# A graph-network kernel: three of ten scaled one-hot copies move from ScalarE to GpSimd

## The reference

```python
a = leaky_relu(sum((xj + ee) * attn, axis=-1), 0.01)   # one logit per edge
m = segment_max(a, dst, num_segments=N)                # the greatest logit of each target node
a = exp(a - m[dst])
denom = segment_sum(a, dst, num_segments=N)
```

## Time and profile before

| | |
|---|---|
| median of 3 runs | 4138.27 us (4135.9 to 4142.09) |
| span of the profiled execution | 4129.6 us; its own time is not listed apart from the runs |
| busy PE, DVE, ACT, POOL over the span | 78%, 59%, 44%, 27% |
| the phase of the change | about 2013 to 2442 us of the span |

### The profile page before, as it was taken

The page is one execution under the profiler, slowest core; times in us unless marked ns, Lnnn a source line. Parts: engine busy times, 40 slices in busy tenths (PEclk is TensorE's granted clock), DMA queues, the critical chain, the costliest instruction groups (busy, mean ns, idle before and its releaser), DMA issues. The chain is left out here.

```text
span 4129.6 us, 85621 instructions
## 1 busy us (share of the span) xinstructions
PE 3235.8 (78%) x18069; PEld 2388.7 (58%) x18070; DVE 2446.4 (59%) x6689; ACT 1829.5 (44%) x6323; POOL 1134.4 (27%) x908
## 2 busy tenths in 40 slices
PE   5666658998887859999543337989996899998988
PEld 4444437887876746767422226878885444544455
DVE  7999988888765643254688868777764200000554
ACT  1888882344455521021688748777772000000111
POOL 1788888888888401101000000000000000000002
PEclk9999999999999979999655559999998999999999
DMA  2444444678788846757565535444331443542047
GB/s 98 125 120 121 122 104 110 186 231 247 224 259 275 292 156 175 211 169 211 174 192 183 170 105 174 125 121 121 105 104 41 150 149 103 199 157 69 1 179 264
DMA packets 436836, 652.83 MB, mean 158 GB/s; under 512 B 101676, under 2 KB 293015, under 8 KB 436610
## 3 DMA queue, kind: packets, MB, share of 16 engines
q1 hardware_dynamic: 353154, 521.08, 40.7%
q10 hardware_dynamic: 53040, 121.95, 8.2%
q0 software_dynamic: 30544, 8.56, 3.0%
HBM read 439.71 MB, written 210.77 MB: 158 GB/s over the span
## 5 line engine op out<-in xcount | busy, mean ns | idle before, releaser
L1065 POOL DMA_INDIRECT slots<-all_B,put_index x800 | 1042.9, 1304 | 343.2 <-issue 338.0
L1950 POOL MEMSET c_T<- 128x28 f32 x1 | 0.1, 148 | 1983.5 <-POOLq L142 1983.5
L1315 ACT ACTIVATE lm_raised<-lm_hot,srt_words 128x125 f32<-128x125 bf16 x1200 | 356.3, 385 | 83.9 <-DVE lm_top L1230 66.9
L2498 DVE TENSOR_TENSOR upd_pre<-upd_po,upd_bias 125x512 f32<-125x512 f32 x25 | 17.3, 691 | 621.7 <-PE upd_po L2429 621.7
L1349 PE MATMUL lm_ps<-lm_v,lm_node 125*128 x1220 | 170.5, 184 | 267.3 <-DVEq L1217 95.2
L2073 PE MATMUL att_ps<-att_right,att_left 128*125 128x125 f32 x2380 | 314.1, 285 | 70.7 <-ACT att_right L2094 57.7
L1036 PE MATMUL put_ps<-put_right_in,put_left_in 128*128 128x125 f32 x2210 | 319.8, 295 | 63.1 <-ACT put_left_in L893 62.8
L2073 PEld LDWEIGHTS att_ps<-att_right,att_left 128*125 128x125 f32 x2380 | 284.5, 190 | 96.3 <-issue 85.4
L1036 PEld LDWEIGHTS put_ps<-put_right_in,put_left_in 128*128 128x128 f32 x2210 | 281.8, 202 | 87.2 <-ACT put_left_in L893 73.2
L2147 DVE SCALAR_TENSOR_TENSOR att_power<-soft_negated,srt_words,att_far 128x125 f32 (+1 forms) x1190 | 321.0, 344 | 3.8 <-ACT att_right L2094 3.3
L1651 PE MATMUL c_po<-c_halves,c_T 125*125 125x512 f32 x1250 | 320.1, 405 | 0.0
(11 more groups left out here) (418 smaller groups left out, 5816.7 us busy)
## 6 DMA issues: line engine op xcount, KB each, us to landing
c_T<-counts SPq DMA_DIRECT2D x255, 312.5 KB, 3.3
pair<-put_T ACTq DMA_DIRECT2D x125, 625.0 KB
att_ring<-hot SPq DMA_DIRECT2D x480, 160.0 KB
gio_T<-pair SPq DMA_DIRECT2D x60, 1250.0 KB, 5.9
hot<-put_hot SPq DMA_DIRECT2D x448, 160.0 KB
all_A<-in_edge_attr_dram SPq DMA_DIRECT2D x100, 448.0 KB
lm_planes<-src_rows SPq DMA_DIRECT2D x123, 320.0 KB, 3.6
counts<-put_T ACTq DMA_DIRECT2D x125, 312.5 KB
```

What stands on the lines that cost most here:

```text
L1065: nc.gpsimd.indirect_dma_start(slots, bass.IndirectOffsetOnAxis(index[:, C * g + j:C * g + j + 1], 0), stage[:, C * g + j, :], None).then_ ...
L1315: ins = nc.scalar.activation(raised[:, j % 2, c * P:(c + 1) * P], hot[:, j, c * S:c * S + P], ACT.Copy, scale=logit[:, ds(G * g + c, 1)])
```

## The change

ScalarE makes the first seven scaled copies of a group (`LIFTS = 7`). GpSimd makes the other three in one instruction: the product of three one-hot matrices, seen as 128 x 3 x 125 with a step of 128 between chunks, with the three logits of each partition, broadcast along the 125 nodes. A new semaphore `hoisted` counts GpSimd's groups and starts at 3, as `lifted` does. DVE waits for it ahead of the maximum and in the filling loop, SP before it reloads a one-hot slot. GpSimd waits for the same three semaphores as ScalarE.

```diff
--- before.py
+++ after.py
@@ -1143,8 +1143,9 @@
         arrived, flipped, copied, written = (s.sem(n) for n in ("arrived", "flipped", "copied", "written"))
         bounded, gathered, floored, cleared = (s.sem(n) for n in ("bounded", "gathered", "floored", "cleared"))
         split, chain_sem = s.sem("split"), s.sem("chain")
-        expanded, looked, summed, ready, lifted, grouped = (
-            s.sem(n) for n in ("expanded", "looked", "summed", "ready", "lifted", "grouped"))
+        expanded, looked, summed, ready, lifted, hoisted, grouped = (
+            s.sem(n) for n in ("expanded", "looked", "summed", "ready", "lifted", "hoisted", "grouped"))
+        LIFTS = 7
         joined, passed, turned, ended = (s.sem(n) for n in ("joined", "passed", "turned", "ended"))
         PZ = 4
 
@@ -1185,6 +1186,7 @@
                         sp.wait_ge(landed[(j + 1) % RING], 16 * (i + (j + 1) // RING) + 16)
                         sp.sem_inc(arrived, 1)
                         sp.wait_ge(lifted, g + 1)
+                        sp.wait_ge(hoisted, g + 1)
                         sp.sem_inc(passed, 1)
                         if not last or j < 3:
                             load_hot(g + 1, j + 1)
@@ -1225,6 +1227,7 @@
                 def greater(g, first):
                     lift = raised[:, ds(g % 2, 1), :].rearrange("p a n -> p (a n)")
                     dve.wait_ge(lifted, g + 4)
+                    dve.wait_ge(hoisted, g + 4)
                     dve.wait_ge(grouped, g + 2)
                     if first:
                         ins = v.tensor_copy(top8[:, :], lift)
@@ -1311,7 +1315,7 @@
                         act.wait_ge(ready, g + 1)
                         act.wait_ge(hot_arrived, g + 1)
                         act.wait_ge(grouped, g + 1)
-                        for c in range(G):
+                        for c in range(LIFTS):
                             ins = nc.scalar.activation(raised[:, j % 2, c * P:(c + 1) * P], hot[:, j, c * S:c * S + P], ACT.Copy,
                                                        scale=logit[:, ds(G * g + c, 1)])
                         ins.then_inc(lifted, 1)
@@ -1319,6 +1323,17 @@
             @block.gpsimd
             def _(pool):
                 nc.gpsimd.memset(ones[:, :], 1.0).then_inc(cleared, 1)
+                pool.sem_inc(hoisted, 3)
+                with pool.Fori(0, turns_of(pool, k)) as i:
+                    for j in range(RING):
+                        g = RING * i + j
+                        pool.wait_ge(ready, g + 1)
+                        pool.wait_ge(hot_arrived, g + 1)
+                        pool.wait_ge(grouped, g + 1)
+                        by_chunk = (lambda t, w: t.rearrange("p (c n) -> p c n", n=w)[:, :, 0:P])
+                        nc.gpsimd.tensor_tensor(by_chunk(raised[:, j % 2, LIFTS * P:], P), by_chunk(hot[:, j, LIFTS * S:], S),
+                                                logit[:, ds(G * g + LIFTS, G - LIFTS)].unsqueeze(2).to_broadcast([L, G - LIFTS, P]), ALU.mult
+                                                ).then_inc(hoisted, 1)
 
             @block.tensor
             def _(pe):
```

## The result

The changed kernel takes 4153.51 us (median of 5 runs, 4150.27 to 4155.78), against 4138.27 us before: 1.0035 times as long, with a 95% interval from 1.0025 to 1.0046. So the change costs 15.2 us. The forecast had the sign and the mechanism; the time lies in the stated range, but the cost is a third of the 43 us that the sum gave.

A forecast was written before the change was run, and what follows sets the result against it. The prediction took DVE to bound the stretch. A 40.4 us hold and a 2.5 us wait, 43 us, raised the span from 4129.6 to 4172.6; 8.7 carried over gave 4181 us, range 4140 to 4228.

The forecast's parts named there:

- DVE sets the pace and ScalarE's relief is worth nothing: Stretch of ScalarE's copies: DVE's 2.95 us step is the bound; gain at most 0.6 us, counted as zero.
- The extra wait, 2.5 us: Ahead of DVE's maximum: one wait more, uncovered, 119 x 0.021 = 2.5 us; bounds 0 and 5 us.
- The product's own time, 0.80 us: GpSimd's product of 375 elements a partition: 0.175 us fixed plus two passes, 0.80 us; bounds 0.49 and 1.30.
- Two-operand instructions are held until a reading product ends: On DVE, L1232, L1218 and L1222 beside GpSimd's product: held like the early cast, until the product ends.
- The hold, 0.43 us in each of 94 steps, 40.4 us: At DVE's sum L1218: start held from 2109.08 to the product's end at 2109.51; 40.4 us in all.
- 94 collisions: DVE's steps where product and L1218 meet: 119 less the 25 after block ends, where L1281 covers the product.
- the held cast: Trace's first microseconds: a DVE cast of 1000 elements took 7.01 us beside a GpSimd memset, 0.68 us with GpSimd idle.
- free window: Time in a DVE step when both operands' way is free: 0.37 us, against the 0.80 the product needs.
- the likeliest case: DVE held by GpSimd's product: 9 to 90 us slower, 4181 us likeliest, own range 4152 to 4228; chance 0.62.
- slower than any row: Rival on GpSimd's product: above 1.30 us it holds L1218 longer; at 2.2 us, 4313 us; chance 0.11.
- ScalarE did not set the pace: Rival it answers: ScalarE's copies set the pace, so the time could fall as far as 4068 us; chance 0.05.
- nothing to be measured: Rival on DVE: two-operand instructions are not held, or the product fits into 0.37 us; 4143 us; chance 0.22.

The follow-up runs named there:

- e4_dry: Against the kernel before: ScalarE still makes all ten copies, GpSimd adds a product of the same shape on tiles of its own; 4153.96 us, 1.0038.
- e11_both: The change with L1218's sums in PSUM and DVE's wait for hoisted at the head of its step; 4141.4 us, 1.0007 to the kernel before.
- e1_wait_only: The change with GpSimd's loop and waits but no product, ScalarE making all ten copies; 4140.97 us, 1.0005 to the kernel before.
- e10_early_wait: The change with DVE's wait for hoisted moved to the head of its step; 4149.92 us, 1.0028 to the kernel before.
- e6_copy: The change with GpSimd copying 1200 elements in the product's place, ScalarE making all ten copies; 4187.21 us, 1.0115 to the kernel before.
- e7_psum_z: The change with L1218's sums in an idle PSUM bank, so L1220 reads one operand from PSUM; 4141.89 us, 1.0006 to the kernel before.
- e5_write: The change with a GpSimd memset of 1320 elements in the product's place, ScalarE making all ten copies; 4143.22 us, 1.0008 to the kernel before.

## Why the prediction was right in sign and wrong in size

- *DVE sets the pace and ScalarE's relief is worth nothing:* right. e4_dry and the change take the same time with ten and with seven copies on ScalarE, and e11_both returns to about the time of before.
- *The extra wait, 2.5 us:* right within its bounds; 3.4 us of idle time, 0.029 us a step, because the instruction went from 21 to 50 ns and DVE's sequencer has no lead there, as its row suggested. Some 1 us of it comes back elsewhere (e1_wait_only). e10_early_wait shows that the place made the price.
- *The product's own time, 0.80 us:* right; 0.81 undisturbed, 0.835 on the average. The reasoning held too: one pass costs e6_copy's copy about 0.84 ns an element (1.19 us undisturbed, less the fixed 0.18), the product's two passes twice that. The estimate of 0.99 us from the Trainium skill's page "GPSIMD Engine Reference", section 3.1, was too long for this product: with two, three and four copies it takes 625, 835 and 1043 ns, 1.67 ns an element.
- *Two-operand instructions are held until a reading product ends:* right, and shown by e4_dry, e6_copy and e7_psum_z. The Trainium skill's page "SBUF — State Buffer", section "Who interferes with whom", says that a DVE instruction with two SBUF inputs contends with a GpSimd instruction that reads SBUF, not with one that only writes. This case agrees: with GpSimd only writing, e5_write, the two-operand L1222 stayed at 170 ns, and with one operand from PSUM, e7_psum_z, L1220 at 169. Why the two-operand sums of the earlier trace rows were not drawn out beside GpSimd's indirect DMAs, no run here shows.
- *The hold, 0.43 us in each of 94 steps, 40.4 us:* this step failed; it measured 0.15 us in 69 steps, 10.4 us. The mechanism was right and the term mis-sized, in three parts. First, "the product runs from 2108.71", the recorded end of L1210: it was let in 0.15 us before that, which with its true length of 0.81 ends it 1.22 us after L1210's start and not 1.35. That is 0.13 us a step. Second, L1218 "is held to 2109.51" and only then begins: it ends 0.02 us behind the product and not its own 0.17, 0.15 us more. Together 0.28 x 69 = 19.3 us. Third, "94 collisions" counted the 25 steps behind a block's first copy, where the sum comes 0.23 us later against the product and escapes: 25 x 0.43 = 10.8 us. The trace of before has this: there L1218 starts 1.19 us after L1210 does, and 0.92 behind a maximum. 40.4 - 19.3 - 10.8 = 10.3.

The first two parts could have been read in the earlier trace rows: the held cast ended 0.54 us behind the memset and takes 0.68 by itself, so it too had begun to count 0.14 us before the holder's recorded end. The free window that the prediction put at 0.37 us was in effect 0.37 + 0.28 = 0.65 us, and two copies, 625 ns, fit into it. That 4153.51 us lies in the likeliest case's own range, 4152 to 4228, is luck: its lower end stood for a product of 0.49 us, and the product took 0.84.

The rivals: the product was never slower than any row, DVE never waited for hoisted, and ScalarE did not set the pace. The rival "nothing to be measured" had the missing hold as its condition; the hold exists.

## What to carry to other kernels

Before work is taken off an engine, look for a row in which another engine waits for it; 100 us of relief bought nothing here because there was none. An instruction moved to GpSimd has a price on DVE if it reads SBUF while DVE reads two operands from there; the price begins only past a free window, so the size of the moved piece decides (two copies cost the wait alone, four cost 29 us), and it can be avoided by taking one of DVE's operands from PSUM, if no other two-operand instruction of DVE meets the moved one. Size such a collision from a case in the trace where one engine really held the other, ends included, and not from the recorded ends of undisturbed instructions.

## What had not been expected of the hardware

- Exclusion ends before the record does: reckoned from undisturbed lengths, the product was let in 0.15 us before L1212's recorded end, and L1220 ended 0.02 us behind the product though it takes 0.17 us alone. The size is not fixed: the memset of e5_write takes 1.20 us undisturbed and ended 1.68 us after L1214's start, which puts its release only 0.07 us before L1214's end.
- A wait instruction on DVE takes 21 ns with one condition and 50 with two, and three more of 50 ns in a row started 0.10 us apart and widened the gap by 0.30 us.
- A memset on GpSimd left two-operand sums alone and held a one-operand subtraction of ten elements, 0.38 in place of 0.23 us, though so small. The Trainium skill's page "SBUF — State Buffer", section "Who interferes with whom", lists tensor_scalar among the instructions that can use both ways into SBUF; the row agrees.
